# When may GpSimd gather the next block of edges: a ring of six buffers, filled six ahead or four ahead

## The reference, cut to what matters

```
h = (x @ W).reshape(n, H, F)                     # 4 heads of 64
a_src = sum(h * att_src);  a_dst = sum(h * att_dst)
e = leaky_relu(a_src[src] + a_dst[dst], 0.2)
ex = exp(e - m[dst]);  denom = segment_sum(ex, dst)
out = segment_sum(h[src] * ex / denom[dst], dst)
```

## Time and profile before

| what | value |
|---|---|
| median of 3 runs | 3565.35 us (3564.39 to 3574.77) |
| the profiled execution | span 4403.2 us, 70224 instructions; the page gives no other time of it |
| busy over the span | PE 3041.5 us (69%), DVE 2365.2 (54%), POOL 2160.0 (49%), ACT 1275.7 (29%) |
| first and last `one_hot` (the edge stage) | 207.4 and 3094.0 us |
| gathers of the stage | 1552 at 954 ns |

### The profile page before, as it was taken

One profiled execution on the slowest core, in us unless ns is written; L12 is line 12 of the kernel. 1 busy time (PEld: TensorE's weight loads), 2 busy tenths in 40 slices (PEclk: granted clock), 3 DMA queues, 4 the chain that ended last, 5 costly groups with the idle time before them and its releaser, 6 DMA issues. The chain is left out here.

```text
span 4403.2 us, 70224 instructions
## 1 busy us (share of the span) xinstructions
PE 3041.5 (69%) x17326; PEld 2470.3 (56%) x17327; DVE 2365.2 (54%) x6486; ACT 1275.7 (29%) x4257; POOL 2160.0 (49%) x2117
## 2 busy tenths in 40 slices
PE   6566666666676776666666777676323349999998
PEld 5444545545555554455555555555323349999997
DVE  7544444444444444545555555555788865555554
ACT  6422222222222222222222222222455523333332
POOL 3255555555555555444444544444066644444444
PEclk9778777878888887878888888888555559999999
DMA  7544444444444444444444444444455724444443
GB/s 262 173 117 117 111 115 112 119 108 111 109 119 111 115 114 117 121 126 121 128 126 122 133 126 125 126 120 111 127 169 186 238 96 71 72 70 72 70 71 55
DMA packets 384652, 529.69 MB, mean 120 GB/s; under 512 B 64276, under 2 KB 323559, under 8 KB 384218
## 3 DMA queue, kind: packets, MB, share of 16 engines
q0 software_dynamic: 114496, 265.49, 25.5%
q1 hardware_dynamic: 185112, 183.84, 14.8%
q10 hardware_dynamic: 84770, 77.19, 5.5%
HBM read 394.80 MB, written 132.72 MB: 120 GB/s over the span
## 5 line engine op out<-in xcount | busy, mean ns | idle before, releaser
L1133 POOL DMA_INDIRECT rows<-node_rows,index x1552 | 1480.9, 954 | 1392.6 <-SPq L1102 930.3
L1411 PE MATMUL ps_sum<-msg,hot 128*128 128x260 f32 x3904 | 1220.7, 465 | 40.0 <-issue 27.9
L1411 PEld LDWEIGHTS ps_sum<-msg,hot 128*128 128x128 f32 x3904 | 853.5, 230 | 198.4 <-issue 45.3
L1391 PE MATMUL ps_hot<-ident_h,hotT 128*128 128x128 bf16 x1952 | 223.5, 247 | 729.7 <-ACT hot L1293 338.6
L1391 PEld LDWEIGHTS ps_hot<-ident_h,hotT 128*128 128x128 bf16 x1952 | 154.3, 110 | 832.8 <-issue 549.4
L1213 DVE TENSOR_TENSOR msg<-rows,ps_w 128x1024 f32<-128x1024 f32 x488 | 596.1, 1222 | 45.1 <-ACT ps_w L1305 29.1
L2140 POOL DMA_INDIRECT out_dram<-big x204 | 352.7, 1729 | 438.3 <-DVE big L2232 390.9
L1195 DVE TENSOR_REDUCE e<-ps_tgt 128x32 f32<-128x96 f32 x488 | 123.3, 253 | 801.2 <-remote 728.2
L1293 ACT ACTIVATE hot<-ps_hot 128x512 f32<-128x512 bf16 x488 | 290.2, 595 | 736.3 <-remote 589.0
L2166 PEld LDWEIGHTS x_ps_hT<-x_rowsT,x_w_now 128*128 128x128 f32 x3264 | 398.0, 192 | 11.5 <-DVE x_w_now L2210 1.1
L2166 PE MATMUL x_ps_hT<-x_rowsT,x_w_now 128*128 128x128 f32 x3264 | 399.1, 276 | 0.7 <-DVE x_w_now L2210 0.7
(11 more groups left out here) (289 smaller groups left out, 4194.9 us busy)
## 6 DMA issues: line engine op xcount, KB each, us to landing
targets<-dst_row SPq DMA_DIRECT2D x391, 128.0 KB
big<-expert_in SPq DMA_DIRECT2D x204, 130.0 KB
rows<-node_rows,index POOLq DMA_INDIRECT x1564
node_rows<-big SPq DMA_DIRECT2D x14, 924.0 KB
turned<-rT SPq DMA_DIRECT2D x14, 896.0 KB, 4.6
area<-turned ACTq DMA_DIRECT2D x98, 128.0 KB
queries<-area ACTq DMA_DIRECT2D x98, 128.0 KB
area<-queries ACTq DMA_DIRECT2D x98, 128.0 KB
```

What stands on the lines that cost most here:

```text
L1133: g.indirect_dma_start(rows[:, j, k, :], None, s.node_rows, bass.IndirectOffsetOnAxis(ap=index[:, b, j * G + k:j * G + k + 1], axis=0)).th ...
L1391: mm = pe.transpose(ps_hot[:, k * P:(k + 1) * P], hotT[:, j % 2, k * P:(k + 1) * P], ident_h[:, :])
L1411: mm = pe.matmul(ps_sum[:, j % 2, 0:SUM], hot[:, j % MSGS, k * P:(k + 1) * P], msg[:, j % MSGS, k, :], start=(k == 0), stop=(k == G - 1))
```

## The change

A constant `IN_FLIGHT` = 4 takes the place of `RING` in GpSimd's wait, and in nothing else.

```
 EARLY = 3
+IN_FLIGHT = 4
 ENTRY = 4
...
-                    if not isinstance(q, int) or q >= RING:
-                        g.wait_ge(slot_free, q - (RING - 1))
+                    if not isinstance(q, int) or q >= IN_FLIGHT:
+                        g.wait_ge(slot_free, q - (IN_FLIGHT - 1))
                         g.sem_inc(s.wait_seen, 1)
```

## The result

| kernel | median us | runs | ratio to before, 95% interval |
|---|---|---|---|
| before | 3568.21 (3564.39 to 3574.77) | 4 | |
| changed | 3724.03 (3715.25 to 3726.48) | 4 | 1.0433 [1.0415, 1.0451] |

The change costs 156 us. The forecast was 60 us (3625), its range ended at 3720. So the direction held, the size did not, and the range missed by 4 us.

The account below looks back on a forecast made before the run. POOL's gather issue was taken to bound the edge stage's first half, PE the second. Losses of 26 (round), 25 (two-pair blocks), 5 (start) and 4 us (second half) made 60 us, 3565 + 60 = 3625 us; range 3540 to 3720, likeliest case 3590 to 3650.

Parts of the forecast that it names:

- The stops of the profile are not in the timed runs: Edge stage: the profile's 838 us over the timed runs are stops caused by recording, so the stage is 2049 us.
- POOL bounds the first half at 5.01 us a block, PE the second: Edge stage: POOL's gathers bound 204 blocks at 5.01 us, PE bounds 184 at 5.7 us; together 2071 us against 2049.
- The round has issue, landing, DVE's step and 0.82 us: Loop over two blocks, from POOL's gathers to `weigh` and back: 8.18 us plus the landing, against POOL's 10.03.
- I take 2.1: Landing of a block's last gather, L: 2.1 us, short end of 2.1 to 3.7; costs 26 us in the first half.
- my own sign of 1.8 to 2.6: Changed profile: the forecast's step is wrong if L, read from `one_hot`'s waits, is under 1.8 or over 2.6 us.
- the 5 of the start: Start of the edge stage: block 4, before gathered at once, now waits for the weighing of block 0; 5 us.
- the term of 25 us for two-pair blocks: First half: 26 two-pair blocks, where DVE needs 6.10 us, each delay POOL by 0.96 us; 25 us.
- PE's 5.7 us a block are above 5.14 ... I estimate at 4 us in all: Second half: PE bounds and hides the loop, apart from runs of single-pair blocks; 4 us.
- The landing is long: Rival on the gathers' landing: L = 2.85 gives 3700 us, the upper bound 3.7 gives 3820 us; chance 0.16.
- No change: Rival: L under about 1.5 us, or PE's jitter hides more; 3565 to 3575 us; chance 0.19.
- Faster: Rival: profile stops are partly real and end earlier with less issued by POOL; 0 to 121 us back, 3505 us; chance 0.18.
- The signs in the profile: Changed profile: short POOL waits at nearly every block, `one_hot` waiting 1 to 2 us for landings, 0.8 us from `weigh` to gather.

Follow-up runs that it names:

- the kernel with five: Changed kernel with IN_FLIGHT = 5 in place of 4, so a block waits for the block five back; 3569.23 us, 1.0004 of before.
- the early `one_hot` with the same ring of six: Kernel before, its ring kept, with `one_hot` waiting for the targets alone and `score` for the rows; 3559.12 us, 0.9965 of before.
- e6: Kernel before with each block's fourth gather left out after the ring's first turn; 3367.85 us, 0.945 of before.
- e4: Changed kernel with IN_FLIGHT = 3 in place of 4, so a block waits for the block three back; 5265.72 us, 1.4763 of before.
- e9: Changed kernel with `one_hot` waiting for the targets alone and `score`, one step later, for the rows; 3569.65 us, 1.0003 of before.

## Why the prediction was right in kind and wrong in size

- *The stops of the profile are not in the timed runs.* Borne out for the timed runs: the kernel with five runs as fast as before and has a span of 3566.5 us without stops. The reason I gave, a cost of recording, stays open. The kernel before alone had stops; the early `one_hot` with the same ring of six had none (span 3558.1 us). I expected the changed kernel's span at 3.8 to 4.3 ms; it was 3713.6, as the stops did not shorten but went.
- *POOL bounds the first half at 5.01 us a block, PE the second.* The first is shown by the kernel with five, where POOL was never held, and fits e6: 190 us less in this half, 186 expected. 1073 us for 855 gathers in the kernel with five is 5.02 us a block.
- *The round has issue, landing, DVE's step and 0.82 us.* Right, term by term in e4, and by taking the DVE step out in e9.
- **The step that failed first is "I take 2.1"** for L. It was 2.48 in the median, inside the bounds of 2.1 to 3.7 that I had given (and inside my own sign of 1.8 to 2.6), and I took the end that was kindest. I argued from the lower load of the DMA engines; but 0.42 was read in a stage slowed by stops, and in this half it is 0.63 with five and 0.55 in the changed kernel. With 2.5 the round is 8.18 + 2.5 = 10.68, 5.34 a block; that is 0.33 over POOL's rate where I had 0.13. Over the 214 blocks of this half it makes 71 us in place of 26. With 31 second pairs at 6.10 - 5.34 us, 24 us, and the 5 of the start that is 100; measured were 98.
- *That this sum fits is in part luck.* In the changed trace a turn of two blocks in this half takes 10.97 us in the mean, against 10.05 with five; half the difference, over 214 blocks, is the whole 98 us. The 95 turns with no two-pair block among the last four take 11.00, the other 114 take 10.95. So the term of 25 us for two-pair blocks is not borne out: they cost nothing beyond the round. Block 4 began 1.5 us late, not 5. The round itself is 0.3 us longer in the mean than its terms; why stays open.
- **The step that failed second is "PE's 5.7 us a block are above 5.14 ... I estimate at 4 us in all"**. It was 49 us. The mean of the half hid how unequal its blocks are. From a block's first `one_hot` to the next block's, the 68 blocks with one pair and no output tile take 3.07 us with five and 3.65 in the changed kernel: 39.5 us. The 38 with one pair and a tile lose 7.3 us. The 68 with two pairs lose 2.7 in all; the 60 of them with a tile take 8.50 and 8.52 us. The short ones now wait for the round, and the long ones don't give that time back. `one_hot` waited 49 times there, against 19. As the long ones, where PE has most to do, are no slower, the lower clock of this half (0.96 against 0.98) is not the cause either.
- *The rivals.* "The landing is long" had the right cause and, with L = 2.85, the nearer time (3700). The nearness is luck: its landing was too long (2.85 against 2.48) and its second half too cheap (10 us against 49). "No change" is out. "Faster" is out: no stops were there to shorten. My range was 4 us short, because it ended at 3720, between this rival's two prices.
- *The signs in the profile.* The 0.82 us came as said. POOL's waits are short, but real at 172 of 388 blocks, not at nearly every one. `one_hot` waits 2.2 us at a time in 229 of 488 pairs, as forecast to some 1 to 2 us; but this sign tells nothing, as with five it waits 187 times and 346.3 us. What tells the kernels apart is whether POOL is held.

## What to carry to other kernels

A ring's depth is a time round a loop: add up issue, landing, the consumer's step up to the last read, and the hand-overs, divide by the number of blocks the wait allows, and compare with the issuing engine's own rate. Where a later engine is the bound, do it block by block and not with a mean over the stage: the short blocks lose what the long ones don't give back. Look at what is in the loop only through program order: here a consumer's step that had no need of the rows stood behind their landing, and freeing it cut the price of the shorter lead from 156 us to 10. Measure the landing in the traffic it will have; one taken in a quieter or an artificially slowed stage is too short.

## What the runs showed of the hardware that I had not expected

- An indirect gather of 128 rows of 1056 bytes landed 1.88 us after its issue ended, in the median, when the blocks came singly (e4), and 2.48 us in a stream with other loads beside it (the changed kernel).
- POOL starts a gather 0.78 to 0.82 us after the semaphore or `weigh` that frees it, in place of 0.30 us in an unbroken stream: by these two figures a wait that ends just as the gather before it does costs half a us.
- The profiled execution of one kernel (before) was 838 us longer than its timed runs; those of the changed kernel and of the kernel with five agreed within a few us. A span must be set beside the times before a stretch of it is priced.
